# 128-row expert tiles, first and second products in alternation, and 512- plus 256-column second products, in a cross-attention and mixture-of-experts kernel

## What is computed

```python
logits = jnp.einsum('bsh,eh->bse', x, Wr)
probs = jax.nn.softmax(logits, axis=-1)
top_v, top_i = jax.lax.top_k(probs, K)
top_v = top_v / jnp.sum(top_v, axis=-1, keepdims=True)
for e in range(E):
    w_e = jnp.sum(jnp.where(top_i == e, top_v, 0.0), axis=-1)
    h = jnp.einsum('bsh,mh->bsm', x, W1[e]) + b1[e]
    h = jax.nn.gelu(h, approximate=False)
    y = jnp.einsum('bsm,hm->bsh', h, W2[e]) + b2[e]
    out = out + y * w_e[..., None]
```

## Time and profile before

| | us |
|---|---|
| median of 3 runs | 484.67 |
| the runs | 478.1, 484.67, 484.67 |
| profiled execution, its own time | 480.82 |
| its span, first to last instruction | 478.9 |
| share of TensorE's clock granted, mean over the span | 0.944 |
| busy PE, PEld | 411.0, 317.9 |
| busy DVE, ACT, POOL | 319.3, 198.8, 142.2 |

### The profile page before, as it was taken

How to read it: one execution, slowest core, us unless ns; L and a number is a source line. 1 busy time by engine, 2 the same in 40 slices (tenths; PEclk the granted TensorE clock), 3 DMA queues, 4 the chain that set the end, 5 groups by cost and what they waited for, 6 DMA issues and landing times.

```text
span 478.9 us, 9857 instructions
## 1 busy us (share of the span) xinstructions
PE 411.0 (86%) x2876; PEld 317.9 (66%) x2877; DVE 319.3 (67%) x895; ACT 198.8 (42%) x339; POOL 142.2 (30%) x133
## 2 busy tenths in 40 slices
PE   3989899779898654039999999999999999999991
PEld 1345547436465543028888888888888888888880
DVE  2104755876769575917777777777777777777771
ACT  0214956775667464203443343333333434343330
POOL 8200300304253446800333222222223333222222
PEclk9999999999989975559999999999999999999997
DMA  7930037227534715240233332222222233332211
GB/s 241 327 117 0 22 117 247 90 88 237 203 121 130 258 65 167 78 144 1 46 50 67 53 53 44 46 44 44 44 44 44 44 49 62 56 54 44 44 22 23
DMA packets 32482, 43.46 MB, mean 91 GB/s; under 512 B 3088, under 2 KB 27920, under 8 KB 32336
## 3 DMA queue, kind: packets, MB, share of 16 engines
q1 hardware_dynamic: 19840, 27.24, 19.5%
q0 software_dynamic: 8880, 12.69, 13.8%
q10 hardware_dynamic: 3744, 3.31, 2.0%
HBM read 28.45 MB, written 14.78 MB: 90 GB/s over the span
## 4 chain that ended last, share of the span: by engine, by line
PE 73%; DVE 11%; ACT 4%; issue 4%; DMA 4%; POOL 2%; SPq 1%; POOLq 1%; DVEq 0%; ACTq 0%
PE o_ps L653 25%; PE s_ps L633 12%; PE t_ps L633 12%; PE proj L473 5%; PE s_ps L507 4%; PE o_ps L526 4%; PE proj L621 3%; PE proj L465 3%; DVE w2l L953 2%; PE proj L494 2%; POOL rows L404 2%; DMA xt<-rows 2%; PE proj L481 2%; PE t_ps L517 1%; DMA w2l<-ctxT 1%
## 5 line engine op out<-in xcount | busy, mean ns | idle before, releaser
L436 POOL DMA_INDIRECT out<-y,idx x46 | 72.5, 1576 | 196.7 <-DVE y L1189 189.7
L826 ACT ACTIVATE g<-s_ps,b_sb,down 128x256 f32<-128x256 f32 x92 | 46.9, 560 | 157.1 <-PE s_ps L633 157.1
L653 PE MATMUL o_ps<-w2h,gl 128*128 x368 | 100.3, 273 | 0.0
L653 PE MATMUL o_ps<-w2h,gh 128*128 x368 | 100.3, 273 | 0.0
L653 PE MATMUL o_ps<-w2l,gh 128*128 x368 | 100.3, 273 | 0.0
L1157 DVE TENSOR_SCALAR gh<-g,up 128x512 f16<-128x512 f32 x92 | 44.8, 486 | 40.9 <-ACT g L826 40.1
L1159 DVE SCALAR_TENSOR_TENSOR gl<-g,up,gh 128x512 f16<-128x512 f32 x92 | 69.1, 751 | 3.3
L826 ACT ACTIVATE g<-t_ps,b_sb,down 128x256 f32<-128x256 f32 x92 | 46.9, 559 | 13.5 <-PE t_ps L633 13.5
L404 POOL DMA_INDIRECT rows<-send,place x32 | 39.1, 1222 | 34.2 <-DVE place L1010 25.6
L653 PEld LDWEIGHTS o_ps<-w2l,gh 128*128 128x128 f16 x368 | 36.0, 98 | 4.2
L653 PEld LDWEIGHTS o_ps<-w2h,gl 128*128 128x128 f16 x368 | 36.0, 98 | 4.2
(11 more groups left out here) (160 smaller groups left out, 681.8 us busy)
## 6 DMA issues: line engine op xcount, KB each, us to landing
staged<-W1T SPq DMA_DIRECT2D x8, 1024.0 KB
staged<-W2T SPq DMA_DIRECT2D x8, 1024.0 KB
xt<-rows SPq DMA_DIRECT2D x23, 260.0 KB, 2.7
...
```

Of the source, the lines that this page charges most:

```text
L436: pool.indirect_dma_start(out=out, out_offset=bass.IndirectOffsetOnAxis(ap=idx[:, u, r:r + 1], axis=0), in_=y2[:, u, r, :], in_offset=None ...
L653: i = nc.tensor.matmul(y_ps[r][:, 0:D], l[:, m, r * P:(r + 1) * P], w[:, bass.ds(e, 1), m * D:(m + 1) * D].rearrange("p a n -> p (a n)"), ...
L826: i = nc.scalar.activation(g[:, m, :], h_ps[s][:, (m % MQ) * TR:(m % MQ + 1) * TR], ACT.Gelu, bias=b1_sb[:, bass.ds(e, 1), m:m + 1].rearra ...
```

## The change

- A tile has 128 rows (TR = P), so TILES = (4096 + 8 * 127) // 128 = 39. The matmuls of the first product have 128 moving columns; there are 48 of them in each tile, as before.
- The halves of the second weight stand side by side in one tensor w2, so that gh by (w2h, w2l) is one matmul of 512 columns into a full bank and gl by w2h one of 256 onto its first half. DVE adds the two halves of the bank (lines 1223 and 1227 of the changed kernel), one operation more for 128 rows than before.
- The products alternate on PE: in the period of tile t it computes slice m of the first product of tile t + 1 and then slice m - 2 of the second product of tile t. The rows are turned two tiles ahead.
- ACT takes the high part of the turned rows instead of DVE. g, gh, gl and the turned rows have two buffers, xt has eight. DVE splits g in halves instead of quarters.
- The gate of a row taken twice is zero now instead of its place being a spare row; the token number travels with the row as an integer and is the scatter's index. Each tile has one scatter, which waits until the one before it has landed.
- The loops on PE, DVE, SP and POOL have a body of 8 tiles; PE and DVE run it 4 times, with 5 tiles written out ahead and 2 behind. On PE each pass of the loop begins with two more reads of an expert. ACT's loop stays at 2 tiles.

```diff
-TR = 2 * P
+TR = P
 REGION = TR + N
 TILES = (2 * N + E * (TR - 1)) // TR
 UNITS = 2 * E
 RING = 3
-XR = 2
+XR = 8
 QUARTERS = 4
 MQ = MC // QUARTERS
+LAG = 2
+HEAD = 5
+TAIL = HEAD + XR * ((TILES - 2 - HEAD) // XR)
+HALVES = 2
+MH = MC // HALVES
...
-        w2h = sb("w2h", [P, E, MC * D], F16)
-        w2l = sb("w2l", [P, E, MC * D], F16)
+        w2 = sb("w2", [P, E, MC, 2, D], F16)
...
-        g = sm("g", [P, MC, TR])
+        g = sm("g", [P, 2, MC, TR])
-        xt = sm("xt", [P, XR, 2, ROW])
-        xh = sm("xh", [P, DC, TR], F16)
-        xl = sm("xl", [P, DC, TR], F16)
-        gh = sm("gh", [P, MC, TR], F16)
-        gl = sm("gl", [P, MC, TR], F16)
+        xt = sm("xt", [P, XR, ROW])
+        xs = sm("xs", [P, 2, DC, 2, TR], F16)
+        gh = sm("gh", [P, 2, MC, TR], F16)
+        gl = sm("gl", [P, 2, MC, TR], F16)
         y1 = sm("y1", [P, 2, D])
...
+        y2 = sm("y2", [P, 2, D])
+        gates = sm("gates", [P, 2, 3])
...
-        xT_ps = proj[0]
+        xT_ps = proj
...
+                    sp.wait_ge(added, t * 16 - (XR - 1) * 16)
...
+                sp.dma_start(xt[:, slot, :], rows[bass.ds(first, TR), :]).then_inc(xt_in[slot], 16)
+            for t in range(XR - 1):
+                load_rows(t, t)
...
-                    pool.wait_ge(added, t * 32)
...
+                    pool.wait_ge(added, t * 16)
+                pool.wait_ge(y_ready, t + 1)
+                pool.sem_inc(scattering, 1)
+                pool.indirect_dma_start(out=out, out_offset=bass.IndirectOffsetOnAxis(ap=xt[:, slot, D + 3:D + 4].bitcast(I32), axis=0),
+                                        in_=y2[:, slot % 2, :], in_offset=None, compute_op=ALU.add).then_inc(added, 16)
...
             def turn_tile(t, slot):
-                wait_rows(pe, t, slot)
+                pe.wait_ge(xt_in[slot], rows_landed(t, slot))
                 for c in range(DC):
...
+                    i = nc.tensor.transpose(xT_ps[slot % 2][:, c * TR:(c + 1) * TR],
+                                            xt[:, slot, c * P:(c + 1) * P], ident[:])
                 i.then_inc(turned, 1)
-            def hidden(t, e):
-                pe.wait_ge(xs_ready, t + 1)
+            def expert(t):
+                return pe.value_load(expert_of[0:1, bass.ds(t, 1)], min_val=0, max_val=E - 1)
+            def hidden(t, m, slot, e):
+                bank = h_ps[m // MQ]
+                if m % MQ == 0 and (not isinstance(t, int) or t):
+                    pe.wait_ge(g_ready, t * QUARTERS + (m // MQ + 1 - QUARTERS))
+                for k, (w, half) in enumerate(((w1h, 0), (w1h, 1), (w1l, 0))):
+                    for c in range(DC):
+                        at = c * M + m * P
+                        i = nc.tensor.matmul(bank[:, (m % MQ) * TR:(m % MQ + 1) * TR],
+                                             w[:, bass.ds(e, 1), at:at + P].rearrange("p a n -> p (a n)"),
+                                             xs[:, slot % 2, c, half, :], start=(k == 0 and c == 0),
+                                             stop=(k == 2 and c == DC - 1))
+                if m % MQ == MQ - 1:
+                    i.then_inc(h_full, 1)
+            def second(t, m, slot, e):
+                if m % MH == 0:
+                    pe.wait_ge(gs_ready, t * HALVES + (m // MH + 1))
+                nc.tensor.matmul(y_ps[slot % 2][:], gh[:, slot % 2, m, :],
+                                 w2[:, bass.ds(e, 1), m, :, :].rearrange("p a k n -> p (a k n)"),
+                                 start=(m == 0), stop=False, skip_group_check=True)
+                i = nc.tensor.matmul(y_ps[slot % 2][:, 0:D], gl[:, slot % 2, m, :],
+                                     w2[:, bass.ds(e, 1), m, 0, :].rearrange("p a n -> p (a n)"),
+                                     start=False, stop=(m == MC - 1), skip_group_check=True)
+                if m == MC - 1:
+                    i.then_inc(y_full, 1)
+            def tile(t, phase, ahead, e_before, e):
+                e_next = None
+                if ahead > 0:
+                    e_next = expert(t + 1)
+                    pe.wait_ge(xs_ready, t + 2)
                 for m in range(MC):
...
+                    if ahead > 0:
+                        hidden(t + 1, m, (phase + 1) % XR, e_next)
+                    if ahead > 1 and m == LAG:
+                        turn_tile(t + 2, (phase + 2) % XR)
+                    if m >= LAG:
+                        if m == LAG and (not isinstance(t, int) or t >= 2):
+                            pe.wait_ge(y_biased, t - 1)
+                        second(t, m - LAG, phase, e)
+                    elif not isinstance(t, int) or t:
+                        second(t - 1, m + MC - LAG, (phase - 1) % XR, e_before)
+                return e, e_next
             turn_tile(0, 0)
+            turn_tile(1, 1)
             pe.wait_ge(low_ready, UNITS)
...
+            experts = (None, expert(0))
+            pe.wait_ge(xs_ready, 1)
+            for m in range(MC):
+                hidden(0, m, 0, experts[1])
+            for t in range(HEAD):
+                experts = tile(t, t, 2, *experts)
+            with pe.Fori(HEAD, TAIL - XR + 1, XR) as t:
+                experts = (expert(t - 1), expert(t))
+                for k in range(XR):
+                    experts = tile(t + k, (HEAD + k) % XR, 2, *experts)
+            experts = (expert(TAIL - 1), expert(TAIL))
+            for t in range(TAIL, TILES):
+                experts = tile(t, t % XR, min(2, TILES - 1 - t), *experts)
+            for m in range(MC - LAG, MC):
+                second(TILES - 1, m, (TILES - 1) % XR, experts[0])
...
+            def take_high(t, u):
+                act.wait_ge(turned, t + 1)
+                if not isinstance(t, int) or t >= 2:
+                    act.wait_ge(h_full, t * QUARTERS - QUARTERS)
+                nc.scalar.activation(xs[:, u, :, 0, :], xT_ps[u][:, 0:DC * TR].rearrange("p (c n) -> p c n", c=DC),
+                                     ACT.Copy).then_inc(xs_high, 1)
+            def gelus(t, u, ahead):
                 e = act.value_load(expert_of[0:1, bass.ds(t, 1)], min_val=0, max_val=E - 1)
                 for s in range(QUARTERS):
                     act.wait_ge(h_full, t * QUARTERS + (s + 1))
                     for m in range(s * MQ, (s + 1) * MQ):
-                        i = nc.scalar.activation(g[:, m, :], h_ps[s][:, (m % MQ) * TR:(m % MQ + 1) * TR], ACT.Gelu,
+                        i = nc.scalar.activation(g[:, u, m, :], h_ps[s][:, (m % MQ) * TR:(m % MQ + 1) * TR], ACT.Gelu,
...
                     i.then_inc(g_ready, 1)
-            gelus(0)
-            with act.Fori(1, TILES - 1, 2) as t:
+                    if s == 1 and ahead:
+                        take_high(t + 1, 1 - u)
+            take_high(0, 0)
+            take_high(1, 1)
+            gelus(0, 0, False)
+            with act.Fori(1, TILES - 2, 2) as t:
                 gelu_table()
-                gelus(t)
+                gelus(t, 1, True)
                 act.wait_ge(warmed, (t + 3) // 2)
-                gelus(t + 1)
+                gelus(t + 1, 0, True)
+            gelus(TILES - 2, 1, True)
+            gelus(TILES - 1, 0, False)
...
+            def take_low(t, u):
                 dve.wait_ge(xs_high, t + 1)
...
+                nc.vector.tensor_tensor(xs[:, u, :, 1, :], xT_ps[u][:, 0:DC * TR].rearrange("p (c n) -> p c n", c=DC),
+                                        xs[:, u, :, 0, :], ALU.subtract).then_inc(xs_ready, 1)
+            def expert(t):
+                return dve.value_load(expert_of[0:1, bass.ds(t, 1)], min_val=0, max_val=E - 1)
+            def split(t, u, s, e):
                 by = up[:, bass.ds(e * 2, 1), 1:2].rearrange("p a n -> p (a n)").bitcast(F32)
...
+                dve.wait_ge(g_ready, t * QUARTERS + (s + 1) * (QUARTERS // HALVES))
+                m = slice(s * MH, (s + 1) * MH)
+                nc.vector.tensor_scalar(gh[:, u, m, :], g[:, u, m, :], by, None, ALU.mult).then_inc(g_high, 1)
+                dve.wait_ge(g_high, t * HALVES + (s + 1))
+                nc.vector.scalar_tensor_tensor(out=gl[:, u, m, :], in0=g[:, u, m, :], scalar=by, in1=gh[:, u, m, :],
                                                op0=ALU.mult, op1=ALU.subtract).then_inc(gs_ready, 1)
-            def mark(t, u, slot):
+            def mark(t, slot):
+                u = slot % 2
...
+                nc.vector.scalar_tensor_tensor(out=gates[:, u, 2:3], in0=gates[:, u, 0:1], scalar=gates[:, u, 1:2],
+                                               in1=fresh[:, bass.ds(t, 1)], op0=ALU.add, op1=ALU.mult).then_inc(marked, 1)
+            def result(t, u, e):
+                dve.wait_ge(y_full, t + 1)
+                nc.vector.scalar_tensor_tensor(out=y1[:, u, :], in0=y_ps[u][:, 0:D], scalar=undo[:, bass.ds(e, 1)],
+                                               in1=b2_sb[:, bass.ds(e, 1), :].rearrange("p a n -> p (a n)"),
+                                               op0=ALU.mult, op1=ALU.add).then_inc(y_high, 1)
```

(21 more changed lines are left out.)

191 lines of the change are left out of this document (58 added, 133 removed).

## The result

The changed kernel takes 497.94 us (median of 4, 495.76 to 503.81) where the kernel before took 481.64 (median of 4, 478.1 to 484.67) on the same chip: a ratio of 1.033, 95% interval 1.020 to 1.045. It is 3.3% slower. The prediction said 486, inside a range of 470 to 503, and held "slower by over 2%" at 0.30; 497.94 lies in the range, and the centre was 12 us low.

The account below looks back on a forecast made before the run. The prediction took PE's columns to bound the kernel before and PE's sequencer the changed one: expert part 259.9 against 256.4 us, start and end nothing, about +3, giving 484 from the profiled execution and 488 from the median; forecast 486, range 470 to 503.

Parts of the forecast that it names:

- What bounds the kernel before: Expert part: PE's own stream of matmul columns sets 11.1 us a tile; register instructions are hidden by the sequencer's lead.
- Columns: PE's array: 0.055 us per 128-column matmul, 5.5 us a tile; by columns alone the expert part takes 42 us less.
- rival (b): PE: weight loads don't hide under 128-column matmuls, 0.080 us each, 6.7 us a tile, 495 us in all; chance 0.08.
- The register step: PE's sequencer: register instructions don't halve with the columns, need 6.4 us a tile against the array's 5.5, and become the bound.
- The bracket of the prediction: PE's sequencer: range for the pace of the dense instruction mix, 0.45 to 0.52 us a slice, 5.9 to 6.7 a tile.
- Rival (a): PE: register work overlaps matmul issue, PE keeps the columns' pace, DVE's 5.7 to 5.8 sets the period; 455 us, chance 0.17.
- Rival (c): PE and DVE: DVE's result and split come too late for slice 6, so PE stands each tile; 504 us, chance 0.17.
- the loop heads: PE: five loop heads or exits, each two more value loads (1.4 us) and a branch (0.2 to 0.3), 8.5 us together.
- Start: Expert part up to the loop: first product at the lower clock 5.1 us, written-out tiles 5.9 each; uncovered waits, including the end's, 3.5.
- The sum: Expert part: the terms for looped tiles, heads, written-out tiles, first and last product and waits give 259.9 us against 256.4.
- Rival (d): PE, DVE or both: the 8-tile loop body is fetched again at each pass; +6 us, 492 in all, chance 0.05.
- Start and end at nothing: Before and after the expert part: first rows 0.7 us less, last scatter about 3.1 after the last matmul as now; together nothing.

Follow-up runs that it names:

- e8: The kernel before, with expert 0's weights at constant addresses in every product on TensorE: 479.45 us, ratio 0.999 to the kernel before.
- e2: The changed kernel with expert 0's weights at constant addresses, so no address is computed on TensorE: 463.20 us, ratio 0.967 to the kernel before.
- e5: The changed kernel with VectorE's split of a tile's second half moved ahead of the previous tile's result: 492.35 us, ratio 1.021 to the kernel before.
- e6: The changed kernel with the edits of e5 and e3 together: 475.24 us, ratio 0.985 to the kernel before.
- e9: e7 without the bounds check of the expert's number on TensorE: 456.88 us, ratio 0.942 to the kernel before.
- e3: The changed kernel with four of TensorE's 40 address instructions a tile replaced by constant addresses: 495.49 us, ratio 1.038 to the kernel before.
- e7: The changed kernel with the edits of e4 and e5, and b2's load issued behind the first row load: 469.65 us, ratio 0.968 to the kernel before.
- e4: The changed kernel with TensorE's 39 tiles all written out instead of looped: 483.45 us, ratio 1.012 to the kernel before.

## Why the prediction was right or wrong

The forecast was 486, no change to speak of, and the kernel came out 3.3% slower: the mechanism and its price for a looped tile were right, and what stands at the edges (start, heads, end) was priced too low every time.

**What bounds the kernel before: right.** Columns; e8 shows that its register instructions are free.

**Columns and rival (b): right.** 0.055 for 128 columns, 0.22 for 512, 5.5 a tile (e2: 5.51). The 0.080 of rival (b) is excluded. The Trainium skill ("TensorE: Matmul & The Clock Gate", section "Back-to-back issue gap") gives 81 ns for such a stream; this trace shows four in 0.22 us, and the measurement decides.

**The register step: right, and the one that mattered.** 6.4 was forecast, 6.38 measured, 6.32 without the round. In e5, six tiles show 162 FUSED_REGOPS, 130 ALU_OP and six value loads with a check each: by the gaps between their starts 27 x 0.129 + 21.7 x 0.110 + 0.36 + 0.08 = 6.3 a tile (gaps add up to the period whatever sets it; that they are the bound is shown by e2, e6 and e9). The bracket of the prediction, 0.45 to 0.52 a slice, gives 6.0 to 6.6 by its own sum and not 5.9 to 6.7; 6.38 lies in both. One picture of it was wrong: I looked for slices 0.60 to 0.65 apart with the array idle in between. Sequencer and array are nearly even in a slice, and the array's idle time gathers at the value load.

**Rival (a), the columns' pace with VectorE's 5.7: fell** (e2, e3). VectorE's 5.7 was too high; it keeps up with 5.51.

**Rival (c), the round: the step that failed.** (The round: `y_full`, VectorE's result and split, `gs_ready`, TensorE's slices 6 to 1, the next `y_full`.) The prediction had VectorE answer 3.2 us after `y_full` and TensorE ask 3.5 after it, a room of 0.3, priced at nothing. VectorE needs 3.33. How soon TensorE asks where nothing holds it is to be seen in e5:

```profile
386.24 0.27 PE L659 MATMUL o_ps<-w,gl 128*128 x1
...
389.58 0.38 PE L656 MATMUL o_ps<-w,gh 128*128 x1
```

3.34 us. So the two are even, and the room was nothing. In a plain tile that costs 0.06 us. But I had priced the loop heads on TensorE alone, and VectorE's head lies in the round: 8.39, 7.57, 7.45 and 7.45 us behind the four heads are 5.3 over 4 x 6.38, of which about 0.9 is the lower clock in the first. The price of this rival, 504, was too high, since it made every tile pay. And at the end, where nothing else fills the array, the round shows bare:

```profile
489.33 0.39 PE L656 MATMUL o_ps<-w,gh 128*128 x1 [1.66 <-DVE gl L1204]
```

**Start: wrong, by a step that was not there.** The prediction gave the parts to the loop 5.1 + 5 x 5.9 and, with those at the end, 3.5 of waits. The start took 41.2, 6.6 over the 34.6. 4.8 is the wait for the first split, which hung on b2's load: the diff shows that load moved from behind two row loads to behind seven, and I costed the row loads' size and not their number on SP's queue. e7 shows it. The 6.8 us at the lower clock that go with the wait are some 1.7 more, as an estimate (0.9 for 3.4 us at the head; in e4, whose stretch is 3.4 us, the two tiles around the wait take 17.75 us instead of 18.61). The prediction had asked that the clock stay near 0.98; it took the lower level for the first product alone, which was dear by 1.2, for the clock rose at 219.7. The five tiles at 6.12 or more instead of 5.9 are 1.1.

**The sum again.** Forecast and measured: to the loop 34.6 and 41.2; loop with its exit 213.3 and 220.2 (heads' tiles +5.3, the first pass's tiles 6.5 instead of 6.38 +1.0, the rest the branches); behind the loop 8.5 and 12.6; waits 3.5, which are in the measured parts. 259.9 and 273.9. The chief term, 32 x 6.4 = 204.8, is 204.2; but for the 1.0 of the first pass, the 14 us missed are at edges.

**Rival (d), refetching the body: about right at nothing.** The branch itself takes 0.28 us. The first pass of the loop is 0.15 a tile slower than the later ones, and e7, all written out, has mean register gaps of 0.135 and 0.121 us where e5 has 0.129 and 0.110, with medians that are the same within 0.001; neither is a stall of a microsecond, and what makes the first pass slower stays open. The Trainium skill, "Runtime: NRT & Kernel Launch", section "Instruction fetch mechanics", has a taken branch stall where its target isn't in the current window of two pages, of 256 instructions each, and gives PE's memory 2048 instructions. By the memory's size this loop body fits, and the trace agrees; by the window it would not, and the trace, with 0.28 us from the branch to the next instruction, decides against a stall.

**Start and end at nothing:** the start of the expert part is 210.3 to 212.1 in e2, e3 and e4, where before had 211.8, and from the last matmul to the end of the span it is 501.9 - 490.8 = 11.1 us against 478.9 - 468.2 = 10.7, so that term holds.
